# The attention's four reorderings, and a query projection whose third quarter begins one unit later

## What is computed

```python
x = x + _L0_attn_ref(_layernorm(x, axis=-1), L0_attn_W_qkv, L0_attn_W_out)
...
qkv = jnp.einsum('bse,ef->bsf', x, W_qkv)
qkv = qkv.reshape(batch, seq_len, 3, NUM_HEADS, HEAD_DIM)
q = rotary_embedding(q, seq_len, HEAD_DIM)
k = rotary_embedding(k, seq_len, HEAD_DIM)
scores = jnp.einsum('bqhd,bkhd->bhqk', q, k) * scale
scores = jnp.where(mask, scores, NEG_INF)
weights = jax.nn.softmax(scores, axis=-1)
out = jnp.einsum('bhqk,bkhd->bqhd', weights, v)
```

## Time and profile before

| | |
|---|---|
| median of 3 runs | 2835.35 us (2833.73 to 2835.57) |
| profiled execution, its own time | 2835.77 us |
| its span, first to last instruction | 2834.1 us |
| TensorE busy | 2644.6 us, 93% |
| VectorE, ScalarE, GpSimd busy | 70%, 57%, 53% |
| mean granted TensorE clock | 0.973 of full |

### The profile page before, as it was taken

How to read it: one execution, slowest core, us unless ns; L and a number is a source line. 1 busy time by engine, 2 the same in 40 slices (tenths; PEclk the granted TensorE clock), 3 DMA queues, 4 the chain that set the end, 5 groups by cost and what they waited for, 6 DMA issues and landing times. The chain is left out here.

```text
span 2834.1 us, 51920 instructions
## 1 busy us (share of the span) xinstructions
PE 2644.6 (93%) x16935; PEld 2339.3 (83%) x16935; DVE 1995.9 (70%) x4219; ACT 1617.2 (57%) x3158; POOL 1501.6 (53%) x1680
## 2 busy tenths in 40 slices
PE   7999989999899999899997799999969999999997
PEld 5888878888788888788886677878759999999997
DVE  6677776777777777667776778878856666666665
ACT  3566666666656666666665533333326666666665
POOL 3676745766656766576754334444424444444444
PEclk9999999999999999999999999999979999999999
DMA  5645443535443544444435554445334444444433
GB/s 166 119 109 121 107 122 83 123 101 129 111 105 89 125 105 119 110 99 97 97 85 142 127 167 142 146 140 152 115 131 99 102 75 88 104 104 104 98 58 52
DMA packets 192360, 316.56 MB, mean 112 GB/s; under 512 B 60496, under 2 KB 106224, under 8 KB 189104
## 3 DMA queue, kind: packets, MB, share of 16 engines
q1 hardware_dynamic: 148656, 216.86, 31.3%
q0 software_dynamic: 43520, 97.46, 13.9%
HBM read 241.08 MB, written 75.17 MB: 112 GB/s over the span
## 5 line engine op out<-in xcount | busy, mean ns | idle before, releaser
L1166 ACT ACTIVATE a_pt<-a_PT 128x512 fp32r<-128x512 f32 (+3 forms) x768 | 350.2, 490 | 455.2 <-PE a_PT L1033 449.1
L1311 DVE TENSOR_TENSOR a_pt<-a_PT,a_pt 128x512 fp32r<-128x512 f32 (+3 forms) x768 | 401.4, 550 | 158.4 <-ACT a_pt L1166 154.2
L1301 DVE CUSTOM_DVE_ANT_0 a_S<-a_S,a_mask 128x1024 f32<-128x1024 f32 (+7 forms) x512 | 387.4, 757 | 76.2 <-PE a_S L1022 74.7
L1155 ACT ACTIVATE a_pb<-a_S,a_nmax 128x1024 f32<-128x1024 f32 (+7 forms) x512 | 380.5, 743 | 36.4 <-DVE a_nmax L1301 36.2
L1033 PE MATMUL a_PT<-early_ident,a_pb 128*128 128x128 f32 x2304 | 346.2, 277 | 53.1 <-DVE a_pt L1311 52.6
L1033 PEld LDWEIGHTS a_PT<-early_ident,a_pb 128*128 128x128 f32 x2304 | 277.2, 142 | 114.4 <-issue 60.6
L1050 PE MATMUL a_O<-a_pt,a_v 128*128 128x256 f32 (+1 forms) x2560 | 345.3, 282 | 17.5 <-DVE a_xt L1286 16.0
L1050 PEld LDWEIGHTS a_O<-a_pt,a_v 128*128 128x128 f32 x2560 | 329.4, 193 | 31.0 <-DVE a_xt L1286 24.0
L1021 PE MATMUL a_S<-a_kh,a_qs 128*128 128x512 f32 (+3 forms) x768 | 285.8, 372 | 15.9 <-DMA a_kl<-early_rot 14.3
L2203 POOL DMA_INDIRECT early_stage<-in_we,e_ix x119 | 128.8, 1082 | 275.3 <-issue 140.5
L1022 PE MATMUL a_S<-a_kl,a_qs 128*128 128x512 f32 (+3 forms) x768 | 258.2, 348 | 0.0
(11 more groups left out here) (329 smaller groups left out, 7579.2 us busy)
## 6 DMA issues: line engine op xcount, KB each, us to landing
a_qs<-early_rot SPq DMA_DIRECT2D x256, 128.0 KB, 2.3
a_kh<-early_rot SPq DMA_DIRECT2D x256, 128.0 KB, 2.4
a_kl<-early_rot SPq DMA_DIRECT2D x256, 128.0 KB, 2.3
m_hn<-scr_hs SPq DMA_DIRECT2D x40, 516.0 KB, 3.7
scr_attT<-a_ot SPq DMA_DIRECT2D x256, 64.0 KB, 2.2
early_stage<-in_wqk POOLq DMA_DIRECT2D x31, 512.0 KB, 4.0
m_att<-scr_attT SPq DMA_DIRECT2D x30, 512.0 KB, 4.4
m_rb<-scr_rinv SPq DMA_DIRECT2D x60, 256.0 KB, 5.2
```

The lines of the kernel that those rows point to most:

```text
L1155: act.activation(pb[u % 2][:, 0:cols], S[u % 2][:, 0:cols], ACT.Exp, bias=nmax[:, u % GU:u % GU + 1], scale=-1.0, accum_out=rsum[:, b % 2, ...
L1166: act.activation(pt[u % 2][:, 0, 4 * s:4 * s + m, (qt % 2) * P:(qt % 2 + 1) * P], PT[(k + s) % 2][:, 0:m * P].rearrange("p (k q) -> p k q" ...
L1301: dve.tensor_tensor_reduce(out=sc, in0=sc, in1=mask[:, T - cols:T], scale=-1.0, scalar=-MASKED, op0=ALU.add, op1=ALU.min, accum_out=nmax[: ...
L1311: dve.tensor_tensor(pt[u % 2][:, 1, 4 * s:4 * s + m, q], PT[(k + s) % 2][:, 0:m * P].rearrange("p (k q) -> p k q", k=m), pt[u % 2][:, 0, 4 ...
```

## The change

- `tile_out` runs at the end of the unit in which the tile is turned, no longer early in the unit after; `turn_tile` moves ahead of `turn`.
- The sums use a quarter of `a_O` in place of `a_Z`, leave the rotation `zorder`, and are turned after the unit's first projection steps and inverted at the unit's end; the next product with the values waits for it.
- `x_low` runs one unit after the high half, behind the row maximum; the first of the four pieces moves from place 7 to 8.
- `rope_mult` of quarter 3 runs behind `part_low`; the other quarters stay ahead of it.
- `QSTEPS`: quarter 2's first step moves from entry 5 to entry 6.

```diff
-        QSTEPS = (2, 0, 1, 3, 2, 1, 0, 3, 2, 1, 1)
+        QSTEPS = (2, 0, 1, 3, 2, 0, 1, 3, 2, 1, 1)
...
-            if u == U + 2:
-                return B - 1
...
-            b = sums_turn(u)
-            if b is not None:
-                zorder.append(("s", b, 0))
...
-        XSPLIT = (7, 9, 10, 11)
+        XSPLIT = (8, 9, 10, 11)
...
+                for lag in range(1, 4):
+                    if sums_turn(u - lag) is not None:
+                        pe.wait_ge(s_sums, sums_turn(u - lag) + 1)
                 values(k)
+
+            def turn_sums(b, out):
+                pe.wait_ge(s_exp, GU * G * (b + 1))
+                pe.transpose(out, rsum[:, b % 2, :], ident[:, :]).then_inc(s_sumT, 1)
...
-                b = sums_turn(u)
-                if b is not None:
-                    z_ready(("s", b, 0))
-                    pe.wait_ge(s_exp, GU * G * (b + 1))
-                    pe.transpose(zbank(("s", b, 0))[:, 0:P], rsum[:, b % 2, :], ident[:, :]).then_inc(s_zfull, 1)
+                if u == U + 2:
+                    pe.wait_ge(s_zfree, len(zorder))
+                    turn_sums(B - 1, Z[0][:, 0:P])
                 fill(u, 0)
+                if sums_turn(u) is not None:
+                    pe.wait_ge(s_ofree, values_done(u))
+                    turn_sums(sums_turn(u), O[:, 2 * P:3 * P])
+                for a in range(2):
+                    if tile_in(u, 9 + 4 * a) is not None:
+                        turn_tile(u, tile_in(u, 9 + 4 * a), a)
                 if 2 <= u < U + 2:
                     turn(u - 2)
                 fill(u, 1)
-                for a in range(2):
-                    if tile_in(u, 9 + 4 * a) is not None:
-                        turn_tile(u, tile_in(u, 9 + 4 * a), a)
...
-                for a in range(2):
-                    if tile_in(u, 10 + 4 * a) is not None:
-                        tile_out(tile_in(u, 10 + 4 * a), a)
+                if 0 < u < U:
+                    for p in splits(u - 1):
+                        if p[0] == "x":
+                            x_low(p)
                 for i, j in ends(q_steps(u - 1), 4):
-                    rope_mult(i, j)
-                if sums_turn(u) is not None:
-                    sums(sums_turn(u))
+                    if j < 3:
+                        rope_mult(i, j)
+                if u == U + 2:
+                    sums(B - 1)
                 for n, j in ends(v_steps(u - 2), 8):
                     v_low(n, j)
                 if 2 <= u < U + 2:
                     part_low(u - 2)
-                if u < U:
-                    for p in splits(u):
-                        if p[0] == "x":
-                            x_low(p)
+                for i, j in ends(q_steps(u - 1), 4):
+                    if j == 3:
+                        rope_mult(i, j)
+                if sums_turn(u) is not None:
+                    sums(sums_turn(u))
+                for a in range(2):
+                    if tile_in(u, 9 + 4 * a) is not None:
+                        tile_out(tile_in(u, 9 + 4 * a), a)
```

More of the change, by code:

```diff
@@ L506, in attention_phase @@
         s_rst = rm.sem("rst")
+        s_sumT = rm.sem("sumT")
+        s_sums = rm.sem("sums")
         s_wm = rm.sem("wm")
@@ L726, in store_sums @@
             def store_sums(b):
-                sp.wait_ge(s_zfree, zi[("s", b, 0)] + 1)
+                sp.wait_ge(s_sums, b + 1)
                 sp.dma_start(dram["rinv"][b * QT:(b + 1) * QT, :, :].rearrange("q a (f p) -> (q a f) p", p=P),
@@ L782, in _ @@
             for u in range(U + 6):
-                if u >= U and sums_turn(u - 1) is not None:
-                    store_sums(sums_turn(u - 1))
+                if u == U + 3:
+                    store_sums(B - 1)
                 if values_turn(u - 1) is not None:
@@ L790, in _ @@
                     stack(u // QT + 1)
-                if u < U and sums_turn(u - 1) is not None:
+                if sums_turn(u - 1) is not None:
                     store_sums(sums_turn(u - 1))
@@ L1316, in sums @@
             def sums(b):
-                dve.wait_ge(s_zfull, zi[("s", b, 0)] + 1)
+                dve.wait_ge(s_sumT, b + 1)
                 if b:
                     dve.wait_ge(s_rst, 16 * b)
-                dve.reciprocal(rT[:, :], zbank(("s", b, 0))[:, 0:P]).then_inc(s_zfree, 1)
+                turned = O[:, 2 * P:3 * P] if b + 1 < B else Z[0][:, 0:P]
+                dve.reciprocal(rT[:, :], turned).then_inc(s_sums, 1)
             def out_add(k):
```

## The result

The changed kernel takes 2845.47 us in the median (2840.51 to 2848.0, 7 runs), beside 2835.35 for the kernel before on the same chip: a ratio of 1.0043, 95% interval 1.0032 to 1.0054. It is 12 us slower by the ratio; 9 faster was forecast. The profiled execution took 2845.25, 9.5 more than that of before (2835.77).

What follows compares the result with a forecast made beforehand. TensorE was taken as busiest, only its waits winnable. Terms -12.6 + 4.0 - 0.3 - 9.0 - 7.5 + 14.8 = -10.6, with +1.5 for the clock -9.1: 2826.7 us; range 2813 to 2837.

Steps and rivals of the forecast that it cites:

- tile copies: Places 5 and 29: copies made a unit earlier are ready before the values, 15 x 0.84 = -12.6 us.
- quarter 3's path: From quarter 3's rope_mult to place 16's scores: a chain without slack starts about 0.5 later, +4.0 us; group 0 -0.3.
- sums: Places 4 and 5, three times: the wait for quarter 2's rope_mult goes, one for the reciprocal comes, -9.0 us.
- next batch's x: Places 7 to 12, three batches: x_low no longer blocks VectorE ahead of the row maximum, 2.5 each, -7.5 us.
- moved step: Places 1, 2, 17, 18: transposes wait instead, 0.19 won, 0.70 paid in the next unit, +14.8 us.
- rival (a): Quarter 3's path does not bind, so place 13's gains stay and its costs are not paid: 2814 us; chance 0.13.
- the clock's 1.5: Place 16, eight groups: TensorE's new wait of 1.3 to 2.6 us brings a lower clock, mostly hidden, +1.5 us.
- Rival (b): The moved step's wait really goes: -11.5 in place of +14.8 us, 2800; chance 0.07.
- (d): New waits of 1.07 us at places 1 and 17 lower TensorE's clock, 1.7 each; at half the places 2852; chance 0.10.
- (c): The x pieces give nothing, stopped behind GpSimd or with ScalarE's queue only shifting the wait: 2834 to 2836; chance 0.20.
- The slower side: Measured slower than before, through the clock rival (d) and a little of the moved step's upper bound; chance 0.13.

Runs made afterwards that it cites:

- the kernel with the table alone: Kernel before with only the QSTEPS table changed, a projection step moved from places 1 and 17 to 2 and 18: 1.0067, 2852.39 us.
- the kernel of the four orders: The changed kernel with the old QSTEPS table, so only the reorderings of tile copies, sums, x_low and rope_mult: 0.9976 of the kernel before, 2825.66 us.
- the four parts: Kernel before with one reordering each: tile copies behind part_low 0.9977, quarter 3's rope_mult behind part_low 1.0009, sums 0.9981, x_low 0.9975.

## Why the prediction was wrong

Against the profiled executions -9.1 was forecast and +9.5 came; +7.7 of it lies in the attention. Step by step, by unit lengths:

| step | forecast | after | tried apart |
|---|---|---|---|
| tile copies, places 5 and 29 | -12.6 | -5.2, and +1.95 at 24 and 25 | -11.1 at these places with the copy ahead |
| quarter 3's path, with the clock | +4.0 - 0.3 + 1.5 | +8.6 at 15 and 16, less 2.2 at 12 and 13 | 12 us won when the chain is relieved |
| sums | -9.0 | -9.3 | -9.3 |
| next batch's x | -7.5 | -4.1 | -5.8 |
| moved step, places 1, 2, 17, 18 | +14.8 | +18.5 | +19 by time, +19.7 by unit lengths |

**The step that failed** is "The copy, made at the end of the unit before, is then ready long before the values". The end of the unit is where the copy stands in VectorE's program; it isn't when it runs. Ahead of it is a `part_low` that waits for ScalarE until 0.13 us before the next unit and then takes 1.15, so the copy ended 0.06 us before the values. I had looked at what the values wait for and not at what is queued ahead of the copy. At places 29, and 13, the values still wait 0.29 of the 0.77 before. With the copy ahead of the low part the gain is 0.80 at places 28 and 29 (7.2 in nine) and 0.65 at 4 and 5 (3.9 in six). So of the 7.4 us that were missing, the copy's place made 5.9; the other 1.5 is mostly that 0.84 was too much for place 5, where the values had waited only 0.48 (my 0.84 compared it with a unit that has no tile to turn). Another 2 us were lost at places 24 and 25, which I didn't look at. They are there in both kernels with the copies alone, so they come of the turned tile's new place: standing ahead of the transposes it makes them start 1.86 us into unit 184 instead of 1.65, the low part follows them, and the transposes of unit 185, which wait for it, start 4.03 instead of 3.81 after unit 184 began.

**The moved step** was right in kind and in its releaser: the transposes wait in its place for the first low part behind `rope_mult`, and the step is paid in the next unit, for 0.69 (0.70 forecast). What was mis-sized is the 0.19 that each unit should win. I let the transposes start 0.06 us after the low part, and they start 0.14 to 0.15 after it. So the unit wins 0.08 to 0.09, and at place 17 of the nine groups with a tile nothing, since the values there start 0.06 after the tile's copy (614.12 in the kernel with the table alone, behind a copy that ends at 614.06). The step alone costs 19.7 for 14.8. The +18.5 of after has 1.5 of group 15 in it and is helped by the earlier copy at place 17, which takes 2.4 off in the kernel with the copies behind the low part.

**The x pieces** were mis-sized in the way that the prediction named and did not book. At 772.12 `x_low` starts 0.05 before L839 of GpSimd (2.39 long) and ends at 775.66, that is 1.1 after L839 ends; at 777.52 it starts inside L857 and ends 1.1 after that. Alone it takes 1.20. So 2.3 and 1.4 us of VectorE are lost in each of the three batches, where 1.1 was lost before. The Trainium skill (SBUF — State Buffer, Who interferes with whom) says that a VectorE instruction with two SBUF inputs contends with GpSimd's reads and that the shared ports are an exclusive lock, whose loser stands still; the trace agrees in that VectorE ended 1.1 after GpSimd both times. The page gives the ports to whoever issues first, and here the one that began 0.05 later by the trace held VectorE. By that rule I had worked out -4.5; -4.1 came. The closeness is partly luck, since the 2.5 a batch that it starts from was the half between two bounds, and alone the part gave -5.8.

**The path of quarter 3** was read rightly as a chain of its own that swallows place 13, and rival (a) is refuted. The net of it is 8.6 - 2.2 = 6.4, where 5.2 was forecast. That is near by luck in part: the later start was 0.42 a group for my 0.5, 3.0 in eight; the clock's 1.5 didn't come; 2.6 came from scores that start later behind the last issue, less shorter issues, and 1.0 from place 16 itself (in the kernel with the copies behind the low part too), neither of which I had in the sum. Rival (b), that the step's wait really goes, and (d), the clock, didn't come either: granted 0.975 after and 0.973 before over the span, with waits of 0.9 to 1.1 at places 1 and 17. (c), that the x pieces give nothing, didn't either. The slower side that I gave 0.13 hung on the clock; what came was an ordinary sum of two overrated gains (the copies and the x pieces) and two underrated losses (the moved step and quarter 3's path). The range ended at 2837, since I bounded the moved step (21.7) and not the copy.

Not settled: why the DMAs land late. In groups 4, 5 and 6 of after the scores started 2.9 to 3.6 us after the last issue, 1.75 to 1.9 in all tight groups before; in the kernel of the four orders it is groups 4, 6 and 8 (2.9 to 3.2). And the four parts' times add to more than they gave together.

## What to carry to other kernels

The place of an instruction in an engine's order tells when it may run, not when it does: before you book a gain for a producer that was moved earlier, look up what stands ahead of it on its own engine and what that waits for. Work may be taken out of a unit at a profit only as far as the next bound is away; where two bounds lie within 0.1 us, taking a step out wins next to nothing. When a profile names who ended a wait, ask the program whether that event was needed: here two events fell together, and the view named the one that was not. And when a gain vanishes, look at the longest path across engines and queues: here an edit of GpSimd's order, with no engine near its limit, was worth 16 us to the changed kernel.

## What the hardware showed unexpectedly

Pairs of stacking DMAs on SyncE's queue take 1.23 us to issue as a rule, and 1.88 to 2.64 in 17 of 256 cases of the timeline before. In 13 of the 17 a piece of GpSimd's scan (L909) ran meanwhile, in a quarter of the others (55 of 239). In the timeline after it is 7 of 16 long pairs, and again a quarter of the others. The kernel with the copies ahead, group 5:

```profile
585.71 2.31 POOL L909 TENSOR_TENSOR scan_keys<-scan_keys 128x256 f32<-128x256 f32 x5
...
586.93 2.51 SPq L713 DMA_DIRECT2D a_kh<-early_rot  x2
```

That is a coincidence in time, not a cause shown, and the timeline after weakens it. Whatever the cause, a long pair makes the chain 0.7 to 1.4 us longer where it falls on it, and issues that took 3.7 us more in the eight groups largely explain why copies ahead lost more at places 15 and 16 (9.4) than they won at 12 and 13 (7.3).
